# Low part of y in the weights stage: from GpSimd to VectorE

## What is computed

```
xn = rmsnorm(x, norm_gamma)                       # y in the kernel, before gamma
sn = rmsnorm(slot_embeds, slot_norm_gamma)        # 8 experts x 128 slots
logits = einsum('bnd,esd->bnes', xn, sn)
dispatch = softmax(logits, axis=1)                # over tokens
combine = softmax(logits.reshape(b, n, e * s), axis=-1)
slots = einsum('bnd,bnes->besd', xn, dispatch)
h = gelu(einsum('besd,edh->besh', slots, w1) + b1)
eo = einsum('besh,ehd->besd', h, w2) + b2
out = einsum('bmd,bnm->bnd', eo, combine)
```

## Time and profile before

| | us |
|---|---|
| median of 3 runs | 835.61 (835.45 to 835.63) |
| the profiled execution's own time | 835.44 |
| its span | 833.3 |
| busy: TensorE / VectorE / ScalarE / GpSimd | 826.1 / 643.3 / 548.2 / 86.7 |
| granted clock of TensorE | 1.00 |

### The profile page before, as it was taken

The page is one execution under the profiler, slowest core; times in us unless marked ns, Lnnn a source line. Parts: engine busy times, 40 slices in busy tenths (PEclk is TensorE's granted clock), DMA queues, the critical chain, the costliest instruction groups (busy, mean ns, idle before and its releaser), DMA issues.

```text
span 833.3 us, 14932 instructions
## 1 busy us (share of the span) xinstructions
PE 826.1 (99%) x4866; PEld 717.7 (86%) x4866; DVE 643.3 (77%) x1293; ACT 548.2 (66%) x1078; POOL 86.7 (10%) x103
## 2 busy tenths in 40 slices
PE   8999999999999999999999999999999999999997
PEld 8989999888888888878888888888888888899997
DVE  8788888899999999998867666665766665477776
ACT  5676766657787887689555565555555554568775
POOL 0300000033223334350000000000000000000000
PEclk9999999999999999999999999999999999999999
DMA  6111131102223252225030202020110203066893
GB/s 209 59 51 52 53 99 33 45 28 101 102 94 121 98 192 102 76 77 203 1 102 0 101 1 101 0 98 3 45 55 2 99 1 101 1 217 210 282 292 111
DMA packets 52562, 75.38 MB, mean 90 GB/s; under 512 B 3104, under 2 KB 33696, under 8 KB 52384
## 3 DMA queue, kind: packets, MB, share of 16 engines
q1 hardware_dynamic: 52512, 74.76, 26.8%
HBM read 49.59 MB, written 25.17 MB: 90 GB/s over the span
## 4 chain that ended last, share of the span: by engine, by line
PE 96%; DVE 2%; ACT 1%; issue 1%; DMA 0%; ACTq 0%; DVEq 0%
PE bank L1014 21%; PE bank L1044 13%; PE bank L1086 11%; PE bank L883 10%; PE bank L908 10%; PE bank L1047 7%; PE bank L892 3%; PE bank L750 3%; PE bank L800 3%; PE bank L693 2%; PE bank L773 2%; PE bank L761 2%; PE bank L783 2%; PE bank L715 1%; PE bank L726 1%; PE bank L1022 1%
## 5 line engine op out<-in xcount | busy, mean ns | idle before, releaser
L1014 PE MATMUL bank<-snT,w_r 128*128 128x512 f32 x768 | 194.7, 393 | 0.0
L1495 ACT ACTIVATE act<-bank,b_sb 128x512 f32<-128x512 f32 x128 | 88.0, 687 | 139.3 <-PE bank L1014 138.9
L2121 DVE TENSOR_TENSOR act_r<-act,act_r 128x512 fp32r<-128x512 f32 x128 | 88.3, 691 | 110.7 <-ACT act_r L1500 110.6
L1044 PE MATMUL bank<-w_r,act_r 128*128 128x512 f32 x480 | 173.1, 396 | 0.0
L1014 PEld LDWEIGHTS bank<-snT,w_r 128*128 128x128 f32 x768 | 136.5, 188 | 28.8 <-issue 0.3
L1047 PE MATMUL bank<-w_r,act_r 128*128 128x256 f32 x480 | 134.6, 280 | 0.0
L1044 PEld LDWEIGHTS bank<-w_r,act_r 128*128 128x128 f32 x480 | 90.2, 188 | 21.0
L908 PE MATMUL bank<-disp_r,y_r 128*128 128x512 f32 x384 | 103.4, 406 | 0.4 <-DVE disp_r L1974 0.3
L883 PE MATMUL bank<-yT_r,snT 128*128 128x512 f32 x384 | 99.4, 395 | 0.0
L1047 PEld LDWEIGHTS bank<-w_r,act_r 128*128 128x128 f32 x480 | 90.6, 189 | 4.1
L1086 PE MATMUL bank<-eo_r,comb_r 128*128 128x258 f32 x768 | 92.3, 282 | 0.0
(11 more groups left out here) (203 smaller groups left out, 1311.3 us busy)
## 6 DMA issues: line engine op xcount, KB each, us to landing
combine_scratch<-comb SPq DMA_DIRECT2D x64, 256.0 KB, 2.0
stage<-in_w SPq DMA_DIRECT2D x16, 1024.0 KB, 6.3
stage<-combine_scratch SPq DMA_DIRECT2D x4, 2048.0 KB, 9.0
snT<-combine_scratch SPq DMA_DIRECT2D x4, 2048.0 KB, 9.6
x_scratch<-stage SPq DMA_DIRECT2D x8, 512.0 KB, 3.2
x<-x_scratch SPq DMA_DIRECT2D x8, 512.0 KB, 3.9
x_d<-x_scratch SPq DMA_DIRECT2D x8, 512.0 KB, 9.5
slots_eo<-in_x SPq DMA_DIRECT2D x7, 512.0 KB, 4.4
```

The costliest lines, as they stand in the source:

```text
L1014: last = pe.matmul(hidden_bank(e, i)[:, :], w1_r[q][:, a, k, j * P:(j + 1) * P], sl_r[f][:, c, k, :], start=(n == 0), stop=(n == len(steps ...
L1044: pe.matmul(bank[BH + c][:, :].rearrange("p (w d) -> p w d", w=2), act_r[:, i % RING, 0, c * S:(c + 1) * S], w2_r[q][:, :, j, :], start=(j ...
L1495: act_fn(act[:, i % 2, :], hidden_bank(e, i)[:, :], ACT.Gelu, bias=b1_sb[:, ds(e * KH + i % KH, 1)])\
L2121: v.tensor_tensor(act_r[:, i % RING, 1, :], act[:, i % 2, :], act_r[:, i % RING, 0, :].bitcast(F32), ALU.subtract).then_inc(h_split, 1)
```

## The change

`rest_of_y` goes from GpSimd's block to VectorE's, with the same operands, the same wait on `y_hi` and the same `y_split`; the `nop` ahead of it goes. In batches 1 to 7 VectorE runs it at tiles 4 and 6, behind `rest_of_dispatch` of m-2 and ahead of the next tile's `keep_logits`. In batch 0 the two stand behind `keep_logits` 6 and 7.

```diff
--- before.py
+++ after.py
@@ -617,13 +617,6 @@
                 nc.gpsimd.tensor_scalar(dispatch(b, m), dispatch(b, m), dispatch_cols(b, m)[2], 1.0,
                                         ALU.mult, ALU.mult).then_inc(disp_normed, 1)
 
-            def rest_of_y(b, k):
-                pool.wait_ge(y_hi, b * KD + k + 1)
-                alone(pool)
-                cols = slice(k * P, (k + 1) * P)
-                nc.gpsimd.tensor_tensor(y_r[:, 1, :, cols], y_of(b)[:, :, cols], y_r[:, 0, :, cols].bitcast(F32),
-                                        ALU.subtract).then_inc(y_split, 1)
-
             def centre_out_rows(j):
 
                 pool.wait_ge(w2_summed, j + 1)
@@ -632,8 +625,6 @@
 
             def weights_of(b, centre=False):
                 for m in range(E):
-                    if m in (4, 6):
-                        rest_of_y(b, m // 2 - 2)
                     normalise_dispatch(b, m)
                     if centre and (b, m) in OUT_ROW_AT:
                         centre_out_rows(OUT_ROW_AT.index((b, m)))
@@ -1974,6 +1965,12 @@
                 v.tensor_tensor(disp_r[h][:, 1, :, cols], bank[2 + m % 2][:, :].rearrange("p (t s) -> p t s", t=NT),
                                 disp_r[h][:, 0, :, cols].bitcast(F32), ALU.subtract).then_inc(disp_split, 1)
 
+            def rest_of_y(b, k):
+                dve.wait_ge(y_hi, b * KD + k + 1)
+                cols = slice(k * P, (k + 1) * P)
+                v.tensor_tensor(y_r[:, 1, :, cols], y_of(b)[:, :, cols], y_r[:, 0, :, cols].bitcast(F32),
+                                ALU.subtract).then_inc(y_split, 1)
+
             def shift_of_tokens(b, first):
 
                 dve.wait_ge(min_in_psum, b + 1)
@@ -2014,8 +2011,10 @@
                 invert_sum(0, 5)
                 keep_proj(b, False)
                 keep_logits(0, 6, True)
+                rest_of_y(0, 0)
                 rest_of_dispatch(0, 2)
                 keep_logits(0, 7, True)
+                rest_of_y(0, 1)
                 invert_sum(0, 6)
                 rest_of_dispatch(0, 3)
                 fold_min(0, 3, True)
@@ -2059,6 +2058,8 @@
                         fold_min(b, m, False)
                     if m >= 2:
                         rest_of_dispatch(b, m - 2)
+                    if m in (4, 6):
+                        rest_of_y(b, m // 2 - 2)
                     if m == 5 and not last:
                         make_y(b + 1)
```

## The result

| | before | after |
|---|---|---|
| median of 7 runs, us | 835.54 (835.32 to 835.63) | 838.35 (838.25 to 838.37) |
| profiled execution: time / span, us | 835.44 / 833.3 | 838.33 / 836.6 |

The ratio is 1.0034, with a 95% interval of 1.0023 to 1.0044: slower by 2.8 us. The prediction said 839.0, between 836.3 and 841.0.

What follows compares the result with a forecast made beforehand. TensorE was taken as the bound (busy 99% of the span), VectorE second busiest in the weights stage. Losses per batch summed to 3.35 us on 835.44, giving 838.79; with 0.17 for the median 838.96, said as 839.0, range 836.3 to 841.0.

Steps and rivals of the forecast that it cites:

- fill: TensorE's fill_slots of tile 6, waiting for rest_of_dispatch 3: later by 0.44 us in batch 3, 0.51 in batch 5.
- yT: Low part of yT for the next batch's first logits: 0.31 us more lost in batch 3, 0.27 in batch 5.
- minimum: Last fold_min ahead of TensorE's transpose_min in batch 3: 0.21 us more lost.
- just in time, 0.05: Batches 2 and 4: free time on VectorE absorbs nearly all, yT done as TensorE comes; 0.05 us lost each.
- the sum: Predicted losses of batches 0 to 7 added: 0.45 + 0 + 0.05 + 0.95 + 0.05 + 1.05 + 0.50 + 0.30 = 3.35 us.
- hold-up by GpSimd: Batches 5 to 7: GpSimd's centre_out_rows, reading SBUF, delays the second rest_of_y on VectorE; 0.26 us in each.
- The terms given, 1.20 - 0.5 - 0.2: Batch 0, ahead of rest_of_dispatch 3: 1.20 us added, some 0.5 back from the short fold_min, 0.2 free; predicted 0.45.
- Absorbed: Rival: VectorE is further ahead than starts show, only places where TensorE waits today grow; 1.05 us, 836.7; chance 0.17.
- VectorE becomes the bound: Rival: no room in tiles 4 to 7, every addition lands on TensorE; 9.6 to 13.1 us, 845 to 849; chance 0.10.
- mild form: Milder case of VectorE as the bound: one batch after another loses 0.7 us, giving 841.5; no chance of its own.
- Faster: Rival: VectorE is rid of hold-ups by GpSimd's long operations, TensorE gets back 0.85 us, 834.8; chance 0.05.

Runs made afterwards that it cites:

- three controls: Kernel before with only two semaphores, only GpSimd's loop written out, or only one small VectorE memset more: 835.40, 835.52 and 835.46 us.
- double dose: Changed kernel with every rest_of_y done twice on VectorE, the second waiting for the first: 849.89 us, ratio 1.0177, span 848.1.

## Why the prediction was right, point by point

**What bounds the kernel, and how to price an edit on another engine.** Right. Comparing starts and asking at each consumer what is left of a delay gave 3.35 us for the stage; it lost 3.20. But two errors of 0.6 and 0.8 us, told below, nearly cancelled, so the closeness of the two numbers is luck.

**The operation.** 0.60 from start to start, no wait of its own: right (0.60 in all 16, each 680 ns long, with no idle ahead).

**Batches 3, 2 and 4.** Batch 3 by its steps: fill 0.44 said and 0.52 measured, yT 0.31 and 0.19, minimum 0.21 and 0.16. Batch 2, "just in time, 0.05", lost 0.01 at the first `logits` and 0.12 right after. What the step missed is the weight load of the first matmul. TensorE's weight loads into batch 4, before and after, to be held against the matmuls at 260.62 and 262.09:

```profile
260.40 1.33 PEld L883 LDWEIGHTS bank<-yT_r,snT 128*128 128x128 f32 x6
```

```profile
262.08 0.53 PEld L874 LDWEIGHTS bank<-yT_r,snT 128*128 128x128 f32 x3 [0.46 <-DVE yT_r L1906]
```

Before, the load starts 0.22 us ahead of its matmul; after, load and matmul start together, 0.05 after the first half of yT is done, and the second matmul comes 0.33 later instead of 0.23. So yT is wanted 0.22 earlier than the start of the first matmul tells, and a late one costs 0.07 to 0.13 more, which lengthens the `logits` group from 1.54 to between 1.62 and 1.67. That is so at the head of batches 2 to 7, of batch 3 too: its load waits 0.27 us though its first matmul is 0.01 late. In all it makes 0.6 us that the sum doesn't have. The second half of yT, which I didn't follow either, costs nothing: it is done at 262.63, and the fourth matmul, the first to read it, starts at 262.89. Batch 4 repeats batch 2, as said: of its 0.30 in the table 0.28 belongs to batch 3 (0.12 at the second matmul, 0.16 at the minimum), and its own two steps are again 0.01 and 0.12.

**Batches 5 to 7 and the hold-up by GpSimd.** Batch 5 lost 0.58 at the fill (0.51 said) and 0.26 at yT (0.27), batch 6 0.25 at yT (0.50). What failed is the hold-up. Three terms of 0.26 rested on `centre_out_rows` holding up the second `rest_of_y`. The timelines of VectorE and GpSimd after, in batch 5:

```profile
314.90 0.89 DVE L1945 TENSOR_TENSOR run_min<-run_min,neg_lt 128x512 f32<-128x512 f32 x1
...
316.31 0.68 DVE L1971 TENSOR_TENSOR y_r<-y,y_r 128x512 fp32r<-128x512 f32 x1
```

```profile
314.56 0.70 POOL L617 TENSOR_SCALAR disp<-disp,rz_disp 128x512 f32<-128x512 f32 x1 [3.27 <-DVE rz_disp L1960]
315.24 1.35 POOL L623 TENSOR_SCALAR stage<-stage,w_mean 128x256 f32<-128x256 f32 x1
```

GpSimd's operation of 315.24 lasts to 316.59, and `rest_of_y` runs from 316.31 in its usual 0.68 us. Nor is it slower in batches 6 and 7: the longest of the 16 is 683 ns. Yet `fold_min`, at 314.90, still takes 0.89 beside `normalise_dispatch`. Nor is a short remainder enough to explain it, as GpSimd's and VectorE's rows in batch 7 of the kernel before show:

```profile
367.57 1.28 POOL L624 TENSOR_TENSOR y_r<-y,y_r 128x512 fp32r<-128x512 f32 x1
```

```profile
368.58 0.82 DVE L1954 TENSOR_TENSOR run_min<-run_min,neg_lt 128x512 f32<-128x512 f32 x1
```

There GpSimd's own `rest_of_y` also had 0.27 us left when `fold_min` started, and `fold_min` took 0.82 instead of 0.68. The lengthened `fold_min` rows that I compared, beside `normalise_dispatch` or GpSimd's `rest_of_y`, end 0.53 to 0.55 us after the reported end of GpSimd's operation, so they behave as if held until 0.14 before it. By that measure `rest_of_y` would have taken 0.81 at 316.31; it took 0.68. The Trainium skill ("SBUF — State Buffer", section "SBUF: two separate sides") has the holder keep the pair of SBUF ports that both engines share for its whole instruction; by the reported times that holds, to 0.14 us, for `normalise_dispatch` and GpSimd's `rest_of_y`, and not for the last 0.27 us of `centre_out_rows`. Why that operation differs is open; that its reported end lies further behind its last read is a guess. Without the three terms the sum would be 2.57, so the agreement of 3.35 with 3.20 is luck in part: the weight loads (0.6) filled the gap. The fills of batches 3 and 5 start 0.14 and 0.15 us after VectorE's end, where I used 0.06 from batch 0; that is 0.2 for both, and batch 0 lost 0.1 less than said. Batch 7's 0.23 (0.30 said) are 0.08 at the second matmul at its head, 0.02 at the minimum, and 0.12 at the transpose of a dispatch tile behind it, a place that the sum doesn't name.

**Batches 0 and 1.** Batch 0: 0.45 said, 0.34 measured. (The terms given, 1.20 - 0.5 - 0.2, make 0.5; the short `fold_min` gave back 0.65, from 1.54 to 0.89.) Batch 1: 0.30 gained at the fill and 0.26 lost at yT, as said, and 0.13 more at the second matmul of the `logits`, which the table has in batch 2's row. VectorE and TensorE there, against the earlier trace rows:

```profile
168.45 0.89 DVE L1945 TENSOR_TENSOR run_min<-run_min,slots_eo 128x512 f32<-128x512 f32 x1
...
173.61 0.67 DVE L1965 TENSOR_TENSOR disp_r<-bank,disp_r 128x512 fp32r<-128x512 f32 x1
...
195.31 0.69 DVE L1945 TENSOR_TENSOR run_min<-run_min,neg_lt 128x512 f32<-128x512 f32 x1
```

```profile
174.33 1.66 PE L899 MATMUL bank<-disp_r,y_r 128*128 128x512 f32 x6 [0.41 <-DVE disp_r L1965]
...
199.93 1.66 PE L899 MATMUL bank<-disp_r,y_r 128*128 128x512 f32 x6
```

**The rivals.** "Absorbed" fell: only batches 2, 4 and 6 absorb, and not all of it. "VectorE becomes the bound" is where the double dose lands: from the first dose on, added work is paid in full, so this rival was near. (Its mild form, 8 batches at 0.7, makes 841.2, not 841.5.) "Faster" has its mechanism, and the run without the operation shows that from batch 1 on it was worth 0.5 us once, against 3.3 paid.

**From span to time.** I carried the growth of the span over to the median one to one. The span grew by 3.3 and the time by 2.8, which the 0.4 above explains in number only. With it the forecast of 839.0 would have been 838.6.

## What to carry to other kernels

Before moving work to an engine that is busy for nine tenths of a stage, follow the delay to each consumer, and look in the timeline for the place where that engine catches up: what is pushed past consumers ahead of that place is paid, what reaches it is free, until the slack is used up; then everything is paid. For a group of matmuls take the start of its first weight load, not of its first matmul, as the moment when the operand is wanted. A fraction idle over the stage (here 8% in batches 2 to 6, 10.4 of 137.7 us, against 6 us of new work in them) says nothing of this. Compare batch by batch, too: a sum that comes out right can be two errors. Where a hold-up between two engines costs something in one place only, move one operation, not all.

## What the hardware did that I hadn't expected

- A VectorE subtraction of two SBUF operands wasn't slowed by GpSimd's `centre_out_rows`, which still had 0.20 to 0.27 us to run (the second `rest_of_y` of batches 5 to 7, 676 to 681 ns as in the others), while `fold_min` took 0.82 instead of 0.68 beside a GpSimd subtraction that had 0.27 us left, and 0.89 beside a `normalise_dispatch` that had 0.35 left.
- TensorE's first `logits` matmul of a batch had its weight load 0.22 to 0.23 us ahead of it where its operand was ready. Where it wasn't, load and matmul started within 0.03 us of each other, and the second matmul came 0.31 to 0.33 us after the first instead of 0.23.
- From VectorE's end to TensorE's start it was 0.05 us for the fills of batches 0 and 1 and 0.14 to 0.15 for those of batches 3 and 5, which TensorE runs in a loop, with thresholds from registers. That the loop is the cause wasn't tried.
- The time around the span was 0.4 us shorter in every kernel with a `rest_of_y` on VectorE; three controls didn't bring it out.
